# Decoder block on one core: the state sums of a selective scan, half of each added by an accumulating DMA instead of by TensorE

## The reference, cut to what matters

```
# for each sequence, inner channel e (512), state n (16), position t (256)
h[t, e, n] = exp(dt[t, e] * A[e, n]) * h[t-1, e, n] + dt[t, e] * x[t, e] * B[t, n]
y[t, e]    = sum over n of h[t, e, n] * C[t, n]  +  D[e] * x[t, e]
```

## Time and profile before

| | us |
|---|---|
| median of 3 runs | 1455.17 |
| lowest and highest | 1453.09, 1457.04 |
| the profiled execution | 1455.81 |
| its span in the profile, first to last instruction | 1454.0 |

### The profile page before, as it was taken

The page is one execution under the profiler, slowest core; times in us unless marked ns, Lnnn a source line. Parts: engine busy times, 40 slices in busy tenths (PEclk is TensorE's granted clock), DMA queues, the critical chain, the costliest instruction groups (busy, mean ns, idle before and its releaser), DMA issues.

```text
span 1454.0 us, 17342 instructions
## 1 busy us (share of the span) xinstructions
PE 1267.8 (87%) x6336; PEld 1023.8 (70%) x6336; DVE 1085.2 (75%) x1750; ACT 750.3 (52%) x1637; POOL 278.8 (19%) x239
## 2 busy tenths in 40 slices
PE   3687788899999999999999999999998999899852
PEld 2454556677778787878787777878786878678732
DVE  2799699789977887788959988788778794333216
ACT  1543356365556655664647555665566454534421
POOL 0000124113301242112301231124211330130011
PEclk8877799999999999999999999999999999999967
DMA  4620110201020001100030102010010000000301
GB/s 162 218 76 19 48 38 30 65 1 58 1 99 1 30 30 35 65 30 29 8 92 1 59 0 99 1 30 30 27 66 30 30 8 26 1 0 8 114 0 58
DMA packets 27780, 62.63 MB, mean 43 GB/s; under 512 B 2360, under 2 KB 13720, under 8 KB 27056
## 3 DMA queue, kind: packets, MB, share of 16 engines
q1 hardware_dynamic: 27696, 61.53, 12.6%
HBM read 55.48 MB, written 6.04 MB: 42 GB/s over the span
## 4 chain that ended last, share of the span: by engine, by line
PE 46%; DVE 35%; issue 7%; ACT 7%; POOL 4%; DMA 1%; DVEq 0%; SPq 0%; ACTq 0%; POOLq 0%
PE bank L281 12%; DVE scans L491 10%; PE bank L442 7%; DVE scans L487 6%; PE bank L1066 4%; DVE scans L494 4%; PE bank L1111 4%; PE bank L624 3%; PE bank L1084 3%; PE bank L848 3%; DVE conv L381 2%; DVE nmax L1203 2%; PE bank L842 2%; PE bank L1073 2%; PE bank L579 1%
## 5 line engine op out<-in xcount | busy, mean ns | idle before, releaser
L491 DVE TENSOR_TENSOR_SCAN scans<-scans 128x1024 f32<-128x1024 f32 x128 | 303.2, 2368 | 7.2 <-ACT scans L465 4.9
L465 ACT ACTIVATE scans<-dt,a_neg 128x255 f32<-128x255 f32 x512 | 221.8, 502 | 111.6 <-DVE scans L491 111.4
L442 PE MATMUL bank<-scans,ident 128*128 128x256 f32 x1024 | 261.9, 402 | 19.3 <-DVE scans L494 19.2
L442 PEld LDWEIGHTS bank<-scans,ident 128*128 128x128 f32 x1024 | 198.1, 201 | 56.1 <-DVE scans L494 29.4
L487 DVE TENSOR_TENSOR scans<-conv,BC 128x1024 f32<-128x1024 f32 x128 | 168.3, 1315 | 24.6 <-PE bank L442 20.7
L1147 ACT ACTIVATE ya<-bank,nmax 128x256 f32<-128x256 f32 x256 | 107.0, 469 | 135.2 <-DVE nmax L1203 134.3
L494 DVE TENSOR_TENSOR scans<-scans,BC 128x1024 f32<-128x1024 f32 x128 | 168.9, 1319 | 2.1
L1203 DVE TENSOR_REDUCE nmax<-bank 128x2 f32<-128x512 f32 x128 | 87.4, 683 | 88.4 <-PE bank L1066 88.3
L1084 PE MATMUL bank<-v,ya 128*128 128x65 f32 x1024 | 129.1, 270 | 0.0
L1084 PEld LDWEIGHTS bank<-v,ya 128*128 128x128 f32 x1024 | 125.8, 193 | 1.7 <-issue 0.9
L778 POOL TENSOR_TENSOR wa<-wa 128x512 f32<-128x512 f32 x32 | 61.8, 1940 | 241.0 <-ACT wa L676 240.9
(11 more groups left out here) (255 smaller groups left out, 2192.0 us busy)
## 6 DMA issues: line engine op xcount, KB each, us to landing
BC<-xpj_scratch SPq DMA_DIRECT2D x32, 1024.0 KB, 5.4
xin<-in_x SPq DMA_DIRECT2D x8, 256.0 KB, 2.8
conv<-in_x SPq DMA_DIRECT2D x8, 256.0 KB, 2.8
out<-scans SPq DMA_DIRECT2D x8, 256.0 KB, 2.6
kept_x<-x SPq DMA_DIRECT2D x7, 256.0 KB, 2.0
kept_w<-wa SPq DMA_DIRECT2D x7, 256.0 KB, 2.1
BC<-kept_w SPq DMA_DIRECT2D x1, 1792.0 KB, 9.2
scans<-kept_x SPq DMA_DIRECT2D x1, 1792.0 KB, 13.4
```

What stands on the lines that cost most here:

```text
L442: last = pe.matmul(sums_of(c), ident[:, :], hb[u % 2][:, i, :], start=False, stop=(h == UH - 1 and i == HN - 1), skip_group_check=True)
L465: ins = act.activation(dA[u % 2][:, j, 1:S], dt[b % 2][:, c, 1:S], ACT.Exp, scale=a_neg[:, c, n:n + 1])
L491: dve.tensor_tensor_scan(flat(H[:, :, :]), flat(dA[u % 2][:, :, :]), flat(H[:, :, :]), 0.0, ALU.mult, ALU.add).then_inc(s["a_scan"], 1)
```

## The change

1. PE sums two slices of a unit in place of four. Ahead of that, GpSimd issues one DMA for each unit that reads the upper two state slices of `hb[u % 2]` (128 partitions by 2 KB, 256 KB) and adds them onto the lower two in place. GpSimd waits for `a_hC`; PE waits for the DMA's semaphore, of which there is one for even and one for odd units. There are 128 such DMAs, and GpSimd issued none before.
2. The wide adds leave GpSimd. The rotated queries and keys are added by DVE. Rotary products are two instructions in place of three (the sine table is stored with its sign, and the source is read with its halves swapped). Of the two experts, ACT does one ReLU and DVE does the other together with the add, out of PSUM; the softmax weights of the experts are no longer normalised ahead but in the residual add, which becomes two instructions. The bias of L982 is folded into the weights `w_vo` once.
3. `ORDER` is written anew for all engines: on GpSimd 202 steps in place of 154, 128 of them the DMAs; on DVE 883 in place of 851; on ACT 954 in place of 986; on PE 1100 as before.

```diff
             for u, (h, c) in enumerate(UNITS):
-                pe.wait_ge(*of("a_hC", b, u + 1))
-                for i in range(HN):
-                    last = pe.matmul(sums_of(c), ident[:, :], hb[u % 2][:, i, :], start=False, stop=(h == UH - 1 and i == HN - 1),
+                pe.wait_ge(*of(["a_sum_even", "a_sum_odd"][u % 2], b, 16 * (u // 2 + 1)))
+                for i in range(HN // 2):
+                    last = pe.matmul(sums_of(c), ident[:, :], hb[u % 2][:, i, :], start=False, stop=(h == UH - 1 and i == HN // 2 - 1),
                                      skip_group_check=True)
                 last.then_inc(s["a_y_ps"], 1)
                 yield
...
         def scan_pool(pool, own, b):
+            for u in range(NU):
+                pool.wait_ge(*of("a_hC", b, u + 1))
+                pool.dma_start(flat(hb[u % 2][:, 0:HN // 2, :]), flat(hb[u % 2][:, HN // 2:HN, :]), accum_op=ALU.add).then_inc(
+                    s[["a_sum_even", "a_sum_odd"][u % 2]], 16)
+                yield
...
+            for j in range(4):
+                dve.wait_ge(*of("f_z2_ps", b, j + 1))
+                dve.scalar_tensor_tensor(hid[:, j % 2, :], WB[j % 2][:, :], 0.0, hid[:, j % 2, :], ALU.max, ALU.add).then_inc(s["f_h"], 1)
+                yield
...
-            dve.tensor_tensor(flat(x3[b % 2][:, :, :]), w0[:, :], flat(xb[:, :, :]), ALU.add).then_inc(s["f_res"], 1)
+            for t in range(T):
+                last = dve.scalar_tensor_tensor(x3[b % 2][:, t, :], w0[:, t * D:(t + 1) * D], sc2[:, 2, t:t + 1], xb[:, t, :], ALU.mult, ALU.add)
...
         def x_pool(pool, own, b):
-            for j in range(4):
-                pool.wait_ge(*of("f_r1", b, j + 1))
-                pool.wait_ge(*of("f_r2", b, j + 1))
-                pool.tensor_tensor(hid[:, j % 2, :], hid[:, j % 2, :], r2[:, j % 2, :], ALU.add).then_inc(s["f_h"], 1)
-                yield
...
+                dve.tensor_tensor(out_cos, x, cos, ALU.mult).then_inc(s["t_rot"], 1)
+                dve.tensor_tensor(out_sin.rearrange("p h (b r) -> p h b r", b=2), turned, sin.rearrange("p h (b r) -> p h b r", b=2),
+                                  ALU.mult).then_inc(s["t_rot"], 1)
...
+                    dve.tensor_tensor(keys[:, :, 0:S], cos_k, sin_k, ALU.add).then_inc(s["t_kr"], 1)
+                    dve.tensor_tensor(keys[:, :, S:S + HD], cos_k[:, :, 0:HD], sin_k[:, :, 0:HD], ALU.add).then_inc(s["t_kr"], 1)
...
+                    dve.tensor_tensor(queries[n % 2], rot[n % 2][:, 0, :], rot[n % 2][:, 1, :], ALU.add).then_inc(s["t_ro"], 1)
...
         def y_pool(pool, own, b):
-            for n in range(1, 5):
-                pool.wait_ge(*of("t_rot", b, 6 + 3 * n))
-                if n >= 3:
-                    pool.wait_ge(*of("t_qT_ps", b, n - 2))
-                pool.tensor_tensor(queries[n % 2], rot[n % 2][:, 0, :], rot[n % 2][:, 1, :], ALU.add).then_inc(s["t_ro"], 1)
-                yield
```

More of the change, by code:

```diff
@@ L213, in build @@
         lowT = sb("lowT", [P, 2, S], F32R)
-        x4b, vo, qk, pe_c, pT_c, x1n = [wa[:, 2 * i:2 * i + 2, :] for i in range(6)]
+        vo, qk, pe_c, pT_c, x1n = [wa[:, 2 * i:2 * i + 2, :] for i in range(1, 6)]
+        b_o1 = wa[CTX - P:CTX - P + 1, 8, :]
         tg = wa[:, 0:6, :].rearrange("p (g k) s -> p g k s", g=3)
@@ L735, in x_dve @@
             dve.wait_ge(*of("f_exp", b))
-            own.link(dve.tensor_reduce(sc2[:, 1, :], sm[:, 1, :, :], AX, ALU.add))
-            own.link(dve.reciprocal(sc2[:, 2, :], sc2[:, 1, :]))
-            own.link(dve.tensor_tensor(sm[:, 2, :, :], sm[:, 1, :, :], wide(2), ALU.mult))
-            for i, (score, hit, rank, one) in enumerate([(2, 3, 4, 5), (6, 7, 8, 9)]):
+            own.did(dve.tensor_reduce(sc2[:, 1, :], sm[:, 1, :, :], AX, ALU.add))
+            for i, (score, hit, rank, one) in enumerate([(1, 3, 4, 5), (6, 7, 8, 9)]):
                 top, best = 3 + 2 * i, 4 + 2 * i
@@ L746, in x_dve @@
                 if i == 0:
[L747 removed]
+                    own.link(dve.scalar_tensor_tensor(sm[:, 6, :, :], sm[:, 5, :, :], -2.0, sm[:, 1, :, :], ALU.mult, ALU.add))
+                    own.did(dve.reciprocal(sc2[:, 2, :], sc2[:, 1, :]))
                 yield
[L749 removed]
+            own.link(dve.tensor_tensor(sm[:, 10, :, :], sm[:, 5, :, :], sm[:, 9, :, :], ALU.subtract))
             for t in range(T):
[L751 removed]
+                for i, one in enumerate([9, 10]):
                     own.did(dve.tensor_tensor(low[:, i, t, :].rearrange("p (e r) -> p e r", e=NE),
@@ L762, in x_dve @@
                 dve.wait_ge(*of("l_kept_x", b - 2))
-            dve.tensor_tensor(flat(x3[b % 2][:, :, :]), w0[:, :], flat(xb[:, :, :]), ALU.add).then_inc(s["f_res"], 1)
+            for t in range(T):
+                last = dve.scalar_tensor_tensor(x3[b % 2][:, t, :], w0[:, t * D:(t + 1) * D], sc2[:, 2, t:t + 1], xb[:, t, :], ALU.mult, ALU.add)
+                if t == T - 1:
+                    last.then_inc(s["f_res"], 1)
+                else:
+                    own.did(last)
+            own.wait()
             dve.wait_ge(*of("f_res", b))
@@ L1314, in p_dve @@
             dve.wait_ge(s["prep_pe"], 2)
-            dve.tensor_copy(flat(w_vo[:, :, :]), w1[:, :]).then_inc(s["prep_evac"], 1)
+            own.link(dve.tensor_copy(flat(w_vo[:, :, :]), w1[:, :]))
+            of_ones = w_vo[CTX - P:CTX - P + 1, 1, :]
+            dve.tensor_tensor(of_ones, of_ones, b_o1, ALU.add).then_inc(s["prep_evac"], 1)
             yield
```

151 lines of the change are left out of this document (65 added, 86 removed).

## The result

The changed kernel takes 1489.97 us (median of 4 runs, 1482.08 to 1493.65) against 1454.88 for the kernel before on the same chip. The ratio is 1.0231, 95% interval 1.0201 to 1.0261, so it is slower by 2.3%. The forecast was 1400, and the result lies just inside the upper end of the range, on the other side of the kernel before than the forecast. Its profiled execution took 1490.82 us with a span of 1489.0.

The account below looks back on a forecast made before the run. PE was taken as first bound (92% busy while scans run), DVE a near second (85%). -51 - 25 + 11 - 8 - 3 + 20 = -56 us against 1455.8 gave 1400; own range 1365 to 1435, whole range 1340 to 1490.

Parts of the forecast that it names:

- the one headed PE: PE's sums at L442: 512 fewer records remove 111 us of work, giving -51 on the path and -25 from filled gaps.
- the step headed DMA: Transfer's round trip against DVE's cover between hC and dBx two units later: +20 us in all.
- Rival (d): DVE is the true bound, its idle time from its own order, so PE's relief is lost: 1470 us, chance 0.08.
- DVE, +11: DVE's added adds and ReLUs, +43 us, less 20 of GpSimd contention: net +23 busy, +11 on the path.
- GpSimd, -8: Wide adds leaving GpSimd, which DVE does faster: -8 us on the path, bounds 0 and 58.
- ACT, -3: ACT loses 32 ReLUs of 688 ns, 22 us of work: -3 us on the path.
- L = 4.2 us: DMA round trip from end of hC to the landed sum, taken as 4.2 us between bounds 2.1 and 8.5.
- Rival (b): The DMA round trip is longer than DVE's cover, 116 us missing: 1495 us, chance 0.17.
- Rival (c): GpSimd can't write DMA descriptors while DVE works, each issue 1.9 us late: 1442 us, chance 0.12.
- Rival (a): Full relief: DVE becomes 95% full over a scan stretch of 1053 us: 1352 us, chance 0.15.
- the DMA's 5% of the chain: Sign for wrong: the chain shows a DMA share well above 1%.
- the 50 that counted as right: Sign for right: L487's wait for PE, 20.7 us of idle time before, at most some 50.

Follow-up runs that it names:

- e6: Kernel before with only the wide adds moved off GpSimd: no DMA, four-slice sums, order of before; 1438.59 us, ratio 0.9876.
- e15: e6 run once more, to stand beside other kernels on the same chip; 1441.27 us, ratio 0.9899.
- e10: e6 with PE summing only the lower two slices, no DMA, half of the states left out; ratio 0.9857.
- e2: Changed kernel in its new order without DMA, PE summing only the lower two slices; 1462.03 us, ratio 1.0032.
- e1: Changed kernel in its new order without DMA, PE summing all four slices; 1503.38 us, ratio 1.0303.
- e17: e16 with the order that the change brings; 1467.52 us, ratio 1.0069.
- e13: e6 with both reliefs: PE sums two slices and DVE's hC covers only the lower half of the columns; ratio 0.9547.
- e14: e6 with DVE's hC on only the lower half of the columns, PE still summing four slices; ratio 0.9688.
- e5: Changed kernel with the order of before through the first sequence's head, no DMA and four-slice sums in that sequence; 1442.24 us, ratio 0.9917.
- e9: Whole change in the order of before, PE's letters exactly as before, sums not moved back; 1601.71 us, ratio 1.0989.
- e16: e9 with the DMA accumulating into DRAM; only DVE's next buffer write waits for it, PE sums two slices without waiting; 1454.03 us, ratio 0.9987.
- e8: Whole change in the order of before, with PE's sums moved back; 1539.54 us, ratio 1.0569.
- e7: Kernel before with DMA and two-slice sums, wide adds still on GpSimd, order of before with sums moved back; 1544.69 us, ratio 1.0596.
- e12: As e16, but the DMA to DRAM is plain instead of accumulating; 1440.50 us, ratio 0.9897.
- e11: Changed kernel with the DMA overwriting the lower two slices instead of adding to them; 1473.39 us, ratio 1.0119.

## Why the prediction was wrong

The measured parts beside the terms of the forecast (1 percent is 14.6 us, and each part is uncertain by some 4 us). In the first chain PE is relieved before the order is changed:

```
                                              ratio              us     forecast
moved adds, order of before  (e6, e15)        1 -> 0.989        -16        0   (+11 -8 -3)
PE's relief, order of before (e10)            -> 0.9857          -5      -51
the new order, PE relieved   (e2)             -> 1.0032         +26      -25   (gaps that it fills)
the transfer                 (after)          -> 1.0231         +29      +20
sum                                                             +34      -56
```

In the second the order is changed first, and the transfer is parted:

```
the new order, with 4 sums   (e1)             0.989 -> 1.0303   +60
PE's relief in that order    (e2)             -> 1.0032         -39
DVE's buffer waits           (e17)            -> 1.0069          +5
PE waits for the transfer    (after)          -> 1.0231         +24
```

The step that failed is the one headed PE. It took half of L442's share of the chain (-51) and let the new order fill the gaps (-25), -76 in all. Measured were -5, hardly clear of the noise, and +26: together +21. That is 97 us off; the moved adds gave 16 more than their 0, and the transfer cost 9 more than its 20, which makes the 90 us between forecast and result. Two things in the step were wrong. DVE is right behind PE, so that the relief shows only once DVE is relieved too (20 us, e13 against e14). And the new order had no price. The prediction read from it only DVE's cover; on PE's side it puts other work ahead of the first sequence's sums. With PE relieved its cost is that of the first sequence, 26 us (e2 128.4 us, e10 102.4); in the other seven, losses and gains nearly cancel. Of the 50 us by which the change is behind the moved adds alone, 46 come back when the first sequence gets its old head and its four sums (e5). In every kernel with this order the second sequence takes 17 to 20 us more than in e6 and the seventh 14 to 19; that is located, and its cause was not tested.

In the step headed DMA the size was near (29 against 20) and the question was not complete. It asked only what covers the transfer on DVE, between hC of a unit and dBx of the unit two later. A second engine waits for the same transfer: PE's queue is in order, and what is behind the sum waits with it. The prediction put this question to GpSimd's queue and not to PE's. In the order of before that is most of 146 us (e9 against e16); in the new order, which has the sums late, the wait of PE is worth 24, half of it the round of the first sequence. So the order and the transfer are one price. From the relief alone in the order of before (e10) to the change it is 55 us, and without the new order it would be 104 (e8) to 165 (e9).

- PE, -51 and -25: the relief is worth 3 to 6 us in the order of before, 20 with DVE relieved, 39 in the new order. Half of L442's share of the chain was no gain that the end got. Rival (d), DVE as the true bound, had the mechanism for the order of before. Its time of 1470 was off, since it had DVE's net at +23 and no price for the order.
- DVE, +11, GpSimd, -8, ACT, -3, together nothing: measured -16. The contention with GpSimd's adds was worth its upper bound, 35 us of DVE and not 20: the scan went from 2368 to 2287 ns, dBx from 1315 to 1219, hC from 1319 to 1220, and 128 x (81 + 96 + 99) ns = 35 us. e7, which keeps the adds on GpSimd, keeps the slow scan too (2370). DVE's net is +4 to +8 us of busy time in place of +23.
- L = 4.2 us from the end of hC: 3.7 measured, of which 3.3 from issue to landing. Beside a 1 MB load the landing takes 6.7 to 7.2, so the 3.4 us more for such a collision were about right. The price of this step on DVE alone, +20, was 5 us as measured in the new order (e17) and 6 to 19 in the old (e12, e16), without the sum in the round. The Trainium skill, DMA: Bandwidth & Descriptors, section on the anatomy of one DMA, gave an estimate of 2.6 us; the plain transfer's 2.3 is near it, the accumulating one's 3.3 is not.
- Rival (b) has the right side and, by chance, nearly the right time. Its mechanism is not what happened: it needed an L of 6.4 us or more, and DVE's wait at dBx is 30 us, not 116.
- Rival (c) is wrong: 120 of 128 DMAs were issued within 0.5 us of the end of hC and the last within 1.7, where it had 1.9 us for each, and GpSimd has 3% of the chain (before 4%). Rival (a) is wrong: even with both engines relieved the kernel takes 1388.
- Of what was to show the steps wrong, one sign came clearly, the DMA's 5% of the chain. PE waits for the DMA in its turn, but DVE's wait for PE stayed at 27.5 us, under the 50 that counted as right. The pace of over 6 us a unit tells little: the whole first sequence has 144.4 / 16 = 9.0, but the kernel before had 101.8 / 16 = 6.4, and from unit 2 on it is 6.0 against 5.7. Of the signs for right, DVE over 90% of a shorter scan stretch did not come (947 of 1156 us, 82%).

## What to carry to other kernels

When a step gets a longer latency, ask of every engine that waits for it, not only of the one that reuses the buffer, what stands behind the wait in its queue. Where its step isn't moved back, the work behind it waits too, and moving it back is a change of order that can have a price of its own. When an engine at 92% and one at 85% share a stretch, the relief of the first is worth little until the second is relieved too (here 3 to 6 us of 111, then 20), and the chain's share of a line is not the gain: L442 had 102 us of it. Give a new order a term in the sum, even if it is only a range. Split a change into its parts before keeping it: here a half of it, the moved adds in the old order, is 1.1% faster than the kernel before and 3.3% faster than the whole.

## What the runs showed of the hardware

- An SBUF-to-SBUF transfer of 256 KB issued by GpSimd lands in 2.3 us plain and 3.3 accumulating; an accumulating one into DRAM lands in 4.1. GpSimd is busy for 880 ns with an accumulating issue and 554 with a plain one, as e11's group of issues shows:

```profile
L517 POOL DMA_DIRECT2D scans<-scans x128 | 70.9, 554 | 752.5 <-DVE scans L495 752.4
```

- GpSimd's arithmetic slows DVE, its DMA issues do not: e7, which has both, has a scan of 2370 ns in the mean, and e9, with 128 issues and no wide adds, 2286. The Trainium skill, SBUF — State Buffer, section on who interferes with whom, says that DMAs have ports of their own, apart from the engines'; these two numbers agree.
- With more idle time in front of PE its granted clock was lower. e16 and e9 have the same matmuls in the same order: with 28 us of idle time at the sums the mean clock is 0.919, with 210 us it is 0.878. At 100 to 120 us it was at 0.67 with 18.47 of 20 us busy, and after at 0.57 with 11.51. A sum of four records takes 2.08 us at the half clock and 1.03 to 1.13 at the full one.
